# Cross attention with a routed expert layer: weighted sums of eight heads at the end of every second step

## The reference

```python
# 32 samples: x (32, 112, 256), ctx_768 (32, 375, 192); 16 heads of 64
xn  = layernorm(x)
q   = heads(xn @ Wq);  k, v = heads(ctx @ Wkv)
att = softmax(q @ k.T * 64**-0.5)                 # 112 x 375 for each head
x   = x + concat(att @ v) @ Wproj + bproj
h   = layernorm(x)
p   = softmax(h @ gate_w);  best two of 8 experts, shares normalised
x   = x + sum over the two of share * (silu(h @ gate_e) * (h @ up_e)) @ down_e
```

## Time and profile before

| | |
|---|---|
| Median of three runs | 1486.16 us (1484.12 to 1486.71) |
| Profiled execution, span from the first to the last instruction | 1482.1 us |
| TensorE matmuls busy | 1442.8 us (97%) |
| TensorE weight loads busy | 1284.3 us |
| VectorE busy | 1026.8 us (69%) |
| ScalarE busy | 811.6 us (55%) |
| GpSimd busy | 551.1 us (37%) |
| Granted TensorE clock, mean | 0.995 |

### The profile page before, as it was taken

How to read it: one execution, slowest core, us unless ns; L and a number is a source line. 1 busy time by engine, 2 the same in 40 slices (tenths; PEclk the granted TensorE clock), 3 DMA queues, 4 the chain that set the end, 5 groups by cost and what they waited for, 6 DMA issues and landing times.

```text
span 1482.1 us, 38384 instructions
## 1 busy us (share of the span) xinstructions
PE 1442.8 (97%) x12134; PEld 1284.3 (87%) x12135; DVE 1026.8 (69%) x2665; ACT 811.6 (55%) x2160; POOL 551.1 (37%) x641
## 2 busy tenths in 40 slices
PE   6999999999999999999999999999998899999996
PEld 5898889898888889898988898988886788888885
DVE  5667777676777676767777776777767876666664
ACT  5555555555555555555555555555555565555553
POOL 3524344343434343434343433434326242323332
PEclk9999999999999999999999999999999999999999
DMA  9222222222222222222222222213017233333332
GB/s 272 72 67 69 74 72 74 66 76 66 73 68 77 67 77 76 91 78 78 73 66 73 68 78 66 73 41 101 27 32 283 82 64 58 51 56 51 55 55 27
DMA packets 101379, 113.82 MB, mean 77 GB/s; under 512 B 17260, under 2 KB 88156, under 8 KB 101340
## 3 DMA queue, kind: packets, MB, share of 16 engines
q1 hardware_dynamic: 88172, 94.33, 21.1%
q0 software_dynamic: 12144, 15.66, 6.1%
q10 hardware_dynamic: 1024, 3.34, 0.7%
HBM read 61.37 MB, written 51.93 MB: 76 GB/s over the span
## 4 chain that ended last, share of the span: by engine, by line
PE 92%; DVE 3%; DMA 2%; issue 1%; ACT 1%; POOL 0%; POOLq 0%; ACTq 0%; DVEq 0%
PE bank L1427 26%; PE bank L1370 21%; PE bank L1496 11%; PE bank L1472 11%; PE bank L1462 9%; PE bank L1517 6%; PE bank L1434 4%; DMA out<-y_out,dest_now 2%; PE bank L1676 1%; PE bank L1629 1%; DVE Wgu L1097 1%; PE bank L1544 1%; DVE probT L1228 1%; DMA WkU_whole<-in_L_xattn_Wkv 1%; PE bank L1534 0%
## 5 line engine op out<-in xcount | busy, mean ns | idle before, releaser
L859 ACT ACTIVATE prob<-bank,neg_max 112x375 f32<-112x375 f32 x512 | 298.7, 588 | 135.8 <-DVE neg_max L1222 135.8
L1222 DVE TENSOR_REDUCE neg_max<-bank 112x1 f32<-112x375 f32 x512 | 243.7, 538 | 15.9 <-PE bank L1462 15.7
L1472 PE MATMUL bank<-ident,prob 112*125 112x112 f32 x1536 | 214.5, 274 | 2.7 <-ACT prob L859 2.4
L1472 PEld LDWEIGHTS bank<-ident,prob 112*125 112x125 f32 x1536 | 195.9, 188 | 13.8 <-ACT prob L859 5.0
L1496 PE MATMUL bank<-probT,V 125*64 125x112 f32 x3072 | 176.3, 264 | 2.3 <-DVE probT L1228 1.5
L1496 PEld LDWEIGHTS bank<-probT,V 125*64 125x64 f32 x3072 | 148.8, 137 | 28.7 <-issue 25.5
L1005 DVE TENSOR_TENSOR K_l<-bank,K_h 128x376 fp32r<-128x376 f32 x256 | 140.2, 549 | 48.0 <-ACT K_h L815 41.6
L790 POOL DMA_INDIRECT out<-y_out,dest_now x63 | 97.8, 1552 | 200.9 <-DMA out<-y_out,dest_now 104.5
L1370 PE MATMUL bank<-Wgu,hT_h 128*128 x504 | 165.2, 409 | 2.5 <-DVE hT_l L1288 2.0
L995 DVE COPY V<-bank 125x512 f32<-125x512 f32 x96 | 66.4, 691 | 139.0 <-PE bank L1434 136.0
L813 ACT COPY V<-bank 125x512 f32<-125x512 f32 x96 | 56.3, 587 | 181.9 <-PE bank L1434 179.4
(11 more groups left out here) (209 smaller groups left out, 3867.7 us busy)
## 6 DMA issues: line engine op xcount, KB each, us to landing
bins<-pad_rows SPq DMA_DIRECT2D x29, 1032.0 KB, 5.8
inv_rows<-sums SPq DMA_DIRECT2D x126, 128.0 KB, 2.9
h_in<-bins SPq DMA_DIRECT2D x63, 129.0 KB, 2.4
Wgu<-in_L_ffn_gate_up_w SPq DMA_DIRECT2D x6, 1024.0 KB, 7.7
y_sb<-in_ctx SPq DMA_DIRECT2D x32, 187.5 KB, 2.7
y_sb<-in_ctx SPq DMA_DIRECT2D x62, 93.8 KB, 2.6
x_sb<-in_x SPq DMA_DIRECT2D x16, 224.0 KB, 2.8
x_res<-in_x SPq DMA_DIRECT2D x32, 112.0 KB, 2.4
```

What stands on the lines that cost most here:

```text
L859: nc.scalar.activation(prob[:, j, :], S_ps[j][0:LQ, 0:LKV], ACT.Exp, bias=neg_max[:, j:j + 1], accum_out=row_sum[:, head // HB, head % HB: ...
L1222: nc.vector.tensor_reduce(neg_max[:, j:j + 1], S_ps[j][0:LQ, 0:LKV], AX.X, ALU.max, negate=True).then_inc(max_done, 1)
L1472: last = nc.tensor.transpose(S_ps[j][0:KR, t * LQ:t * LQ + LQ], prob[:, j, t * KR:t * KR + KR], ident[0:LQ, 0:LQ])
```

## The change

In all pairs but the last, the weighted sums of an even step (0 or 2) are held back and computed together with those of the odd step that follows (1 or 3), 48 matmuls in one run. For that the transposed weights have two buffers, one for even and one for odd steps; the second lies where expert 0's weights are loaded, whose load moves from the start of pair 14 to sample 30. The scores of odd steps wait for the copies of the transposed weights themselves. V's products are made in steps 0, 2 and 3. The place "late" is gone: q 2 and q 7 move to "mid" of step 1, q 3 and xT 0 to "early" of step 2. Early items of step 2 go to bank 0, mid items of step 1 as well. VectorE's `norm_x` moves from step 1 to step 0 of even samples, and the low part of step 2's early item stands ahead of `normalise`.

```diff
-PLACES = ("K", "early", "mid", "V", "late")
+PLACES = ("K", "early", "mid", "V")
 def ahead(odd, s):
-    q_at = {(1, 0): (0,), (1, 1): (1,), (1, 2): (2, 3), (1, 3): (4,), (0, 0): (5,), (0, 1): (6,), (0, 2): (7,)}.get((odd, s), ())
-    one = [("q", p) for p in q_at] + {(0, 2): [("xT", 0)], (0, 3): [("xT", 1)]}.get((odd, s), [])
+    q_at = {(1, 0): (0,), (1, 1): (1, 2), (1, 2): (3,), (1, 3): (4,), (0, 0): (5,), (0, 1): (6, 7)}.get((odd, s), ())
+    ones = [("q", p) for p in q_at] + {(0, 2): [("xT", 0)], (0, 3): [("xT", 1)]}.get((odd, s), [])
     places = {"K": [("K", 2 * s), ("K", 2 * s + 1)],
-              "early": one if s < 2 else [],
-              "mid": one[:1] if s >= 2 else [],
-              "V": [("V", t) for t in {0: ((1, 1), (1, 2)), 1: ((0, 0), (0, 1)), 3: ((0, 2), (1, 0))}.get(s, ())],
-              "late": one[1:] if s >= 2 else []}
+              "early": ones[:1] if s < 3 else [],
+              "mid": ones[1:] if s < 3 else ones,
+              "V": [("V", t) for t in {0: ((1, 1), (1, 2)), 2: ((0, 0), (0, 1)), 3: ((0, 2), (1, 0))}.get(s, ())]}
...
-    return {"early": 1, "mid": 0 if s == 2 else 7, "late": 1}[place]
+    return {"early": 0 if s == 2 else 1, "mid": 0 if s == 1 else 7}[place]
...
+def merged(i):
+    return not known(i) or i < NP - 1
...
-        probT = sb("probT", [KR, 4, KT * LQ], F32)
+        probT = [sb("probT", [KR, 4, KT * LQ], F32),
+                 nc.alloc_sbuf_tensor_at("probT_odd", [KR, 4, KT * LQ], F32, offset=shared_from - 4 * KT * LQ * 4)]
...
 (SP's pair)
                 if known(i) and i == NP - 2:
-                    load_expert(sp, 0)
...
                         spread_inverses(b, 0)
+                    if known(i) and i == NP - 1 and not odd:
+                        sp.wait_ge(pv_made, NS * (B - 2))
+                        load_expert(sp, 0)
...
 (ScalarE's pair; turned() of both engines takes the buffer it writes)
                         if there(b, B):
-                            turned(b, s, 2)
-                            turned(b, s, 3)
-                        for k in made_at["late"]:
-                            evacuate(a, k)
+                            to = probT[s % 2 if merged(i) else 0]
+                            turned(b, s, 2, to)
+                            turned(b, s, 3, to)
...
 (VectorE's pair)
+                        to = probT[s % 2 if merged(i) else 0]
+                        if s == 2:
+                            for k in made_at["early"]:
+                                low_part(a, k)
                         if s == 2 and there(b, B):
                             normalise(b, 0)
...
-                        for k in made_at["early"]:
-                            low_part(a, k)
+                        if s != 2:
+                            for k in made_at["early"]:
+                                low_part(a, k)
...
-                        for k in made_at["late"]:
-                            low_part(a, k)
                         if s == 2 and there(b - 2, B):
                             assign(b - 2, odd)
-                        if s == 1 and not odd and (not known(i) or i + 1 < NP):
+                        if s == 0 and not odd and (not known(i) or i + 1 < NP):
                             norm_x(i + 1)
...
 (TensorE: scores, weigh, pair)
                     p = 2 * s + k
+                    if s % 2 and merged(b // 2 if known(b) else b):
+                        pe.wait_ge(probT_second if k else probT_first, 2 * NS * b + 2 * s)
...
-                                      probT[:, 2 * k + r, t * LQ:t * LQ + LQ], start=t == 0, stop=t == KT - 1)
+                                      weights[:, 2 * k + r, t * LQ:t * LQ + LQ], start=t == 0, stop=t == KT - 1)
...
                         if s == 3 and there(b - 1, B):
-                            for k in a.at(odd, 2, "late") if a else []:
-                                pe.wait_ge(lo_done, a.split(k))
+                            if a:
+                                how, n = a.out(a.last_in(1, odd, 2))
+                                pe.wait_ge(out_of[how], n)
                             turn_hn(b - 1, 1 - odd, A_ps[1])
...
                         for k in of_V[1:]:
                             free_bank(a, k)
+                            if s == 2 and there(b - 1, B):
+                                pe.wait_ge(x2_done, b)
...
-                        for k in made_at["late"]:
-                            if there(b - 1, B):
-                                pe.wait_ge(x2_done, b)
-                            make(a, k, i)
...
-                        if there(b, B):
-                            weigh(a, odd, s, b)
+                        if there(b, B) and not merged(i):
+                            weigh(a, odd, s, b, probT[0])
+                        if there(b, B) and merged(i) and s % 2:
+                            weigh(a, odd, s - 1, b, probT[0])
+                            weigh(a, odd, s, b, probT[1])
```

More of the change, by code:

```diff
@@ L860, in weights_of, with turned @@
                                      accum_out=row_sum[:, head // HB, head % HB:head % HB + 1]).then_inc(exp_done, 1)
-            def turned(b, s, j):
+            def turned(b, s, j, to):
                 act.wait_ge(probT_made, H * b + 4 * s + j + 1)
-                nc.scalar.copy(probT[:, j, :], S_ps[j][0:KR, 0:KT * LQ]).then_inc(probT_second, 1)
+                nc.scalar.copy(to[:, j, :], S_ps[j][0:KR, 0:KT * LQ]).then_inc(probT_second, 1)
             def open_gates(b, bank):
@@ L1223, in most, with turned @@
                                         AX.X, ALU.max, negate=True).then_inc(max_done, 1)
-            def turned(b, s, j):
+            def turned(b, s, j, to):
                 dve.wait_ge(probT_made, H * b + 4 * s + j + 1)
-                nc.vector.tensor_copy(probT[:, j, :], S_ps[j][0:KR, 0:KT * LQ]).then_inc(probT_first, 1)
+                nc.vector.tensor_copy(to[:, j, :], S_ps[j][0:KR, 0:KT * LQ]).then_inc(probT_first, 1)
             def pair(i):
@@ L1250, in pair @@
                         if there(b, B):
-                            turned(b, s, 0)
-                        for k in made_at["early"]:
-                            low_part(a, k)
+                            turned(b, s, 0, to)
+                        if s != 2:
+                            for k in made_at["early"]:
+                                low_part(a, k)
                         if there(b, B):
-                            turned(b, s, 1)
+                            turned(b, s, 1, to)
                         for k in made_at["mid"]:
@@ L1474, in turn_prob, with weigh @@
                     last.then_inc(probT_made, 1)
-            def weigh(a, odd, s, b):
+            def weigh(a, odd, s, b, weights):
                 if s == 0:
```

## The result

The changed kernel takes 1511.1 us (median of four runs, 1508.7 to 1512.04), the kernel before 1486.23 us; the ratio is 1.0174 with a 95% interval of 1.0159 to 1.0189. So it is 24.9 us slower, where 23 were forecast, at 1509.

The account below looks back on a forecast made before the run. TensorE's own stream was taken as the bound (70.00 of 70.05 us a pair). Terms -9.6 + 21.6 + 9.8 + 2.1 = +23.9, less about 1, on 1486.2 gave 1509 us; 8 in 10 range 1496 to 1516.

Parts of the forecast that it names:

- The signs that were named: Profile of the changed kernel: step 0 7.3 us, step 2 gap 0.6 to 0.8 ended by K_l, pair 71.5.
- The switches: One matmul shape switch less per merged even step on TensorE: 0.16 us, 60 times, -9.6 us (-6 to -12).
- The bank in step 2: Step 2's early item waits for bank 0 until K's low part is read: 0.72 us, 30 samples, +21.6 us.
- norm_x: In step 0 of even samples it delays V's copy and the maxima: 0.5 us, with the 0.14 slack loss +9.8.
- Rival 1: VectorE's delay is absorbed, 9.8 us shrinks to 2.1: 1502 us, or 1496 at the stall's lower bound; chance 0.14.
- Step 1's slack: Second transposes of every step 1 due 0.28 us sooner, so TensorE waits 0.14; odd samples +2.1 us.
- What was costed at nothing: Odd steps' scores waiting for transposed weights, assign 0.3 us late before step 3, POOL's xn, expert 0's load: no cost.
- rival 3: More harm than counted: 1519 us, or expert 0's load late, at most some 5 us at loop's end; chance 0.08.

Follow-up runs that it names:

- e5_merge01: Kernel before with merging of steps 0 and 1 alone, no place moved; 1481.82 us, ratio 0.9981.
- e9_unmerge: e3_both without the merging: places kept, weighted sums at the end of every step again; 1488.19 us, ratio 1.002 to the kernel before.
- e3_both: Changed kernel with step 2's early item moved to mid with bank 7 and norm_x back in step 1; 1481.53 us, ratio 0.9964 to the kernel before.
- e1_mid: Changed kernel with step 2's early item (xT 0 or q 3) made in mid with bank 7; 1488.34 us, ratio 1.0016 to the kernel before.
- e2_normx: Changed kernel with VectorE's norm_x in step 1 of even samples again; 1504.23 us, ratio 1.012 to the kernel before.
- e7_late: e3_both with step 1's early q block evacuated by ScalarE after the fourth exponential; 1476.8 us, ratio 0.9944 to the kernel before; repeated 1477.17 us.
- e4_merge: Kernel before with the merging alone; ahead, bank_of and norm_x as before; 1489.52 us, ratio 1.0025.
- e10_split: e7_late with assign's last three instructions moved from step 2's end to after step 3's K low parts; 1478.72 us, ratio 0.995 to the kernel before; repeated 1476.6 us.
- e8_exp1: e7_late with ScalarE's second exponential ahead of both K blocks in step 3; 1484.45 us, ratio 1.0002 to the kernel before.

## Why the prediction was right, point by point

- **What bounds.** TensorE's stream and its waits decided the length of the steps in each comparison above. The clock stayed at 1.00 in the loop, the 2.4 GHz level. The signs that were named held: step 0 7.33, step 1 8.52 and 8.08, the wait that ends with K_l in step 2, the first maximum 1.61 after the scores, a pair of 71.65. Step 3 was to grow by 1.15 and grew by 1.08 and 1.07.
- **The switches.** Forecast: 0.16 for each even step. Shown where steps 0 and 1 are merged: 0.14 to 0.19 (e5_merge01, e9_unmerge). The two groups together take 2.45 from the first start to the next scores (617.66 to 620.11), against 1.30 for one alone; so the second costs 1.15, its twelve twos of 0.096, and no more. The Trainium skill (TensorEngine Tiling (Array Packing), Key Properties) says that a change of mode drains the engine, and the runs agree with these 0.14 to 0.19. Where steps 2 and 3 are merged the term was too large: 0.03 and 0.09 in e3_both, because of assign (below). No run takes the merging alone out of the changed kernel. TensorE's timeline of the changed kernel, end of step 1:

```profile
617.66 1.37 PE L1507 MATMUL bank<-probT,V 125*64 125x112 f32 x24
618.86 1.32 PE L1507 MATMUL bank<-probT_odd,V 125*64 125x112 f32 x24
620.11 0.43 PE L1473 MATMUL bank<-K_h,q_h 64*112 64x376 f32 x2
```

- **The bank in step 2.** Forecast 0.72 in each sample, in all 21.6; e1_mid took away 0.79 and 0.73 in step 2, net of step 3 0.69 and 0.68, 1.38 a pair, and 22.8 us of the median.
- **norm_x.** Forecast 0.5 in each even sample beyond the 0.14; e2_normx shows 0.46, and 6.9 us of the median. Rival 1 (absorbed) falls. The prediction's own rows put V's copy 0.9 late, not 0.8 (596.13 + 1.08 is 597.21); it was 0.78. And it counted fifteen such samples: in pair 0, step 1 of the even sample takes 8.07, so there are fourteen.
- **Step 1's slack.** Forecast 0.14; e7_late shows 0.13 and 0.11.
- **What was costed at nothing.** The scores' wait for the transposed weights was free, as said. What e4_merge adds is a second wait at the same scores, for q 7's low part, which the prediction didn't name and the changed kernel avoids by making q 7 in step 1. "ScalarE's first K_h has 0.3 to absorb that" for assign in step 3 was too kind: e9_unmerge and e10_split show that in e3_both 0.05 to 0.14 of each merged step 2 goes there. In the changed kernel itself step 3 is 9.43 and 9.88, against 9.38 and 9.86 in e10_split, so 0.05 and 0.02.
- **The sum.** A pair of the loop is 1.58 longer, and the prediction's terms make 1.59 (23.9 / 15). Part of this closeness is luck. Without the two placements the change was to save 0.36 a pair (0.64 less two times 0.14) and saved 0.28 (e3_both), but as a merging worth 0.46 and places that cost 0.18: the gain was put too high and the cost of the places as well. The bank and norm_x make the rest, 1.38 and 0.49 where 1.44 and 0.51 were forecast.
- **The whole kernel.** From the first scores to the last scores of all pairs the profiles give 1106.6 and 1128.8 us, 22.3 more. The fourteen pairs of the loop are 22.9 longer together and pair 0 is 0.96 longer; the last pair is 1.6 shorter (57.6 to 56.0), which was not foreseen and is not explained here. The two profiled executions differ by 28.0, more than the 24.9 of the medians, because they also differ ahead of the first scores (30.3 and 33.5) and behind the last ones (345.2 and 347.7). Over all profiles here the first scores start between 29.8 and 33.5 and the part behind the last takes 345.2 to 349.5, so no cause is claimed for these differences, and that the median came within 2.1 us of the forecast is in part luck too. The load of expert 0 (rival 3) was not tried by itself; e5_merge01 moves it in the same way and took 1481.82 us, where 1481.5 was expected without any cost for it.

## What to carry to other kernels

A group moved to save a switch of matmul shape is worth the switch, some 0.15 us here, and its cover can be worth more: list what each engine did while the group ran, and which waits it hid (here assign, and q 7's low part in e4_merge), before counting the gain. When an item moves ahead in an in-order stream, look up what last filled its buffer and when that is read out; a bank filled one item earlier cost the full round over two engines, 0.72 us here. And a stall found twice in a kernel (here 0.7 in step 2, 0.3 in e8_exp1) is a placement to fix, not the end of the idea: the merging, with two placements changed, beats the kernel before.

## What the runs showed of the hardware

Nothing in the loop was unexpected in kind. The steadiness was: over the fourteen pairs of the loop steps of one kind differ by a few hundredths of a microsecond, so the median of a step shows 0.03 us in one profile where the timed median needs 2 to 3 us in all. The exception is step 3 of odd samples in the changed kernel and in e2_normx: 9.86 to 9.89 in most pairs, 10.13 to 10.17 in three (four in e2_normx). It is gone with the wait for the bank (9.91 to 9.94 in e1_mid); what makes it is open.
